# Eight-layer block with two expert layers on one core: fixed weight groups kept in SBUF, a state layer without small transfers, moved zeroing, and extra unread products

## What is computed

```python
x = x + cosine_attention(ln(x))       # layer 0, 8 heads of 8
x = x + experts(ln(x))                # layer 1: 160 experts, 8 per token, width 64
x = x + gated_linear_recurrence(ln(x))  # layer 2
x = x + experts(ln(x))                # layer 3, the same weights as layer 1
x = x + state_layer(ln(x))            # layer 4
x = x + channel_mix(ln(x))            # layer 5
x = x + rotary_attention(ln(x))       # layer 6, 16 heads of 8
x = x + channel_mix(ln(x))            # layer 7

def experts(x):
    probs = sigmoid(x @ router_w.T + bias); w, idx = top_k(probs, 8); w = 2.5 * w / sum(w)
    return sum_k w[k] * silu(x @ w_gate[idx[k]].T) @ w_down[idx[k]].T + silu(x @ gs.T) @ ds.T

def state_layer(x):
    u, z = split(x @ W_in + b_in)          # 256 channels each
    c = causal_conv4(u)
    h_t = tanh(c_t @ A + h_{t-1})          # 16 states, 256 steps in turn
    y_t = h_t @ C.T + Dp * c_t
    return (sigmoid(z) * y) @ W_out + b_out
```

## Time and profile before

| | |
|---|---|
| median of 3 runs | 2803.55 us (2802.51 to 2819.82) |
| profiled execution | 2797.68 us; its span in the trace 2795.8 us |
| mean granted clock of TensorE over the span | 0.738 of full speed |
| busy: PE, PEld, DVE, ACT, POOL | 60%, 40%, 49%, 35%, 39% |
| moved by DMA | 383.73 MB, mean 137 GB/s |
| attention of layer 0 | 0 to 205 us |
| experts of layer 1: routing, two halves | 205 to 456, 456 to 676, 676 to 905 us |
| layer 2 and the routing of layer 3 | 905 to 1306 us |
| experts of layer 3, two halves | 1306 to 1532, 1532 to 1770 us |
| state layer | 1770 to 2167 us |
| channel mix, rotary attention, channel mix | to 2217, to 2740, to 2796 us |

### The profile page before, as it was taken

One profiled execution on the slowest core, in us unless ns is written; L12 is line 12 of the kernel. 1 busy time (PEld: TensorE's weight loads), 2 busy tenths in 40 slices (PEclk: granted clock), 3 DMA queues, 4 the chain that ended last, 5 costly groups with the idle time before them and its releaser, 6 DMA issues.

```text
span 2795.8 us, 40361 instructions
## 1 busy us (share of the span) xinstructions
PE 1691.3 (60%) x13716; PEld 1106.9 (40%) x13716; DVE 1381.8 (49%) x3618; ACT 977.7 (35%) x1745; POOL 1080.0 (39%) x1177
## 2 busy tenths in 40 slices
PE   3775333676777454455686767541244468888885
PEld 2554222455555232243454555210022334444453
DVE  3648852322444577666422334552222665666746
ACT  3651001333333321221332323336692433344444
POOL 2000777762761773774770763575000300000001
PEclk9995556878778655555878878755555767899998
DMA  7991114999998111113998999311000000000001
GB/s 227 323 387 50 52 51 163 320 324 302 318 310 262 52 52 46 50 50 109 313 320 276 298 295 293 108 54 37 2 2 2 1 1 1 2 1 1 2 2 31
DMA packets 294229, 383.73 MB, mean 137 GB/s; under 512 B 70816, under 2 KB 163696, under 8 KB 293872
## 3 DMA queue, kind: packets, MB, share of 16 engines
q1 hardware_dynamic: 177280, 160.91, 18.6%
q10 hardware_dynamic: 83984, 153.13, 15.9%
q0 software_dynamic: 32768, 67.17, 7.8%
HBM read 231.64 MB, written 175.11 MB: 145 GB/s over the span
## 4 chain that ended last, share of the span: by engine, by line
PE 37%; DVE 18%; DMA 13%; ACT 12%; issue 8%; POOL 7%; SPq 4%; DVEq 0%; ACTq 0%; POOLq 0%
DMA arena<-expert_blocks 11%; ACT arena L965 5%; PE psum L1994 5%; PE psum L1984 5%; POOL slot_rows L1778 5%; PE psum L448 3%; SPq L1876 3%; PE psum L1957 3%; PE psum L1357 2%; PE psum L1338 2%; PE psum L432 2%; PE psum L1003 1%; PE psum L427 1%; ACT arena L1220 1%; DVE XN L590 1%
## 5 line engine op out<-in xcount | busy, mean ns | idle before, releaser
L1789 POOL DMA_INDIRECT arena<-slot_results,SLOTS x512 | 492.0, 961 | 428.6 <-DMA slot_results<-arena 235.9
L1778 POOL DMA_INDIRECT slot_rows<-arena,SLOTS x512 | 513.5, 1003 | 329.3 <-issue 329.3
L1748 DVE COPY arena<-psum 128x512 f32<-128x512 f32 x288 | 197.5, 690 | 629.7 <-PE psum L1994 624.9
L1984 PE MATMUL psum<-arena 128*64 128x128 f32 x2304 | 231.9, 333 | 225.7 <-DMA arena<-expert_blocks 196.4
L1832 ACT ACTIVATE arena<-psum 128x512 f32<-128x512 f32 x288 | 172.0, 597 | 478.2 <-PE psum L1957 439.9
L169 POOL TENSOR_SCALAR rstd<-mv 128x4 f32<-128x4 f32 x32 | 6.8, 212 | 725.7 <-DVE mv L577 725.2
L1957 PE MATMUL psum<-ident,arena 128*128 128x128 f32 x1152 | 224.7, 327 | 74.0 <-DMA arena<-slot_rows 73.5
L1984 PEld LDWEIGHTS psum<-arena 128*64 128x64 f32 x2304 | 148.0, 162 | 293.0 <-DMA arena<-expert_blocks 215.5
L1994 PE MATMUL psum<-arena 64*128 64x128 f32 x2304 | 248.9, 345 | 8.9 <-DVE arena L1748 8.8
L1994 PEld LDWEIGHTS psum<-arena 64*128 64x128 f32 x2304 | 186.2, 226 | 71.7 <-issue 71.0
L1839 ACT ACTIVATE arena<-psum 128x256 f32<-128x256 f32 x288 | 110.4, 383 | 267.2 <-PE psum L1984 265.6
(11 more groups left out here) (245 smaller groups left out, 3070.3 us busy)
## 6 DMA issues: line engine op xcount, KB each, us to landing
arena<-slot_rows ACTq DMA_DIRECT2D x288, 256.0 KB
slot_results<-arena ACTq DMA_DIRECT2D x288, 256.0 KB
arena<-expert_blocks SPq DMA_DIRECT2D x512, 96.0 KB
arena<-own_blocks SPq DMA_DIRECT2D x160, 256.0 KB
slot_rows<-zeros SPq DMA_DIRECT2D x2, 18432.0 KB, 79.8
own_blocks<-in_expert_w SPq DMA_DIRECT2D x4, 2560.0 KB, 22.6
slot_rows<-arena,SLOTS POOLq DMA_INDIRECT x512, 2.2
arena<-slot_results,SLOTS POOLq DMA_INDIRECT x512
```

The source lines that it names most:

```text
L1748: dve.tensor_copy(YSB[:, p].rearrange("p (c h) d -> p h c d", h=2), psum[:, first:first + 2, 0:256].rearrange("p h (c d) -> p h c d", c=2) ...
L1778: pool.indirect_dma_start(out=slot_rows[h], out_offset=bass.IndirectOffsetOnAxis(ap=slots_of(t, k), axis=0), in_=XNH[:, t], in_offset=None ...
L1789: pool.indirect_dma_start(out=GATHERED[:, t % TPI, k], out_offset=None, in_=slot_results[h], in_offset=bass.IndirectOffsetOnAxis(ap=slots_ ...
L1984: mm = pe.matmul(psum[lo:lo + INTER, 2 + 5 * (p % 2), o:o + P], gate_of(g, q), XSBT[:, p, P * q:P * q + P], start=True, stop=True, skip_gr ...
```

## The change

- **Fixed groups.** The weights of own groups 0 to 28 are put into SBUF (`STAYS`, 29 x 2 KB a partition) once, at the start, straight from the input; `own_blocks` keeps only the other 11. A half still has 72 groups; 43 of them are now brought by SP (`BROUGHT`: 32 by register, 11 own). The 4 buffers EWB serve the brought groups alone, so the load of one waits for the results of the fourth brought group before it, which is 6 or 7 groups back. The order of the own groups is mixed anew so that fixed ones stand evenly among the others. To make room, XSBT has 2 buffers instead of 4 (its writer already waited for the reader two groups back), YSB lies over routing buffers and the buffers of layer 2 over XSB, XSBT and HEB.
- **Two dense products a group.** `inner` issues two bfloat16 products of 256 columns ahead of its own four, into PSUM columns that nothing reads.
- **State layer.** A and C stand in SBUF as 8 padded copies each (A_AT, C_AT), so that PE's product lands on the partitions that the recurrence wants, accumulated in PSUM over four steps, and PE multiplies by C from the same layout. U16, H16 and the 32 small transfers of spreading and collecting go. DVE clears A_AT and C_AT and fills A_AT first (`spread_out`); SP fills C_AT. The sigmoid of the gate is written as tanh of half the argument. Recurrence 0 stands behind steps 4, 5 and 6 (64, 96, 96 steps of tanh). The sums of the last 16 tiles are dealt out anew: one tile in each of steps 0 to 3, four in each of steps 4 to 6.
- **Zeros.** POOL's four memsets for rotary attention stand in the channel mix of layer 5, after `inverse_deviations` of steps 2, 3, 4 and 5. Loops with one body are written out on POOL and PE there.

```diff
-        GROUP_ORDER = sorted(range(GROUPS), key=lambda n: (n + 0.5) / OWN_GROUPS if n < OWN_GROUPS else (n - OWN_GROUPS + 0.5) / MORE_GROUPS)
+        STAYING = 29
+        STAY = {n: n for n in range(STAYING)}
+        OWN_PLACES = sorted(range(OWN_GROUPS), key=lambda n: (n + 0.5) / STAYING if n in STAY else (n - STAYING + 0.5) / (OWN_GROUPS - STAYING))
+        GROUP_ORDER = sorted(range(GROUPS), key=lambda n: (OWN_PLACES.index(n) + 0.5) / OWN_GROUPS if n < OWN_GROUPS else (n - OWN_GROUPS + 0.5) / MORE_GROUPS)
+        BROUGHT = [g for g in range(GROUPS) if GROUP_ORDER[g] not in STAY]
...
-            for g in range(GROUPS):
-                n, p = GROUP_ORDER[g], g % UNROLL
-                if hr or g >= UNROLL:
-                    sp.wait_ge(c_y.sem, c_y.at(hr, 0, g - UNROLL + 1))
+            for m, g in enumerate(BROUGHT):
+                n, p = GROUP_ORDER[g], m % UNROLL
+                if m >= UNROLL:
+                    sp.wait_ge(c_y.sem, c_y.at(hr, 0, BROUGHT[m - UNROLL] + 1))
...
             def inner(g):
                 p = g % UNROLL
+                weights_in(g)
                 pe.wait_ge(c_xt.sem, c_xt.at(hr, 0, g + 1))
                 pe.wait_ge(c_he.sem, c_he.at(hr, 0, g - 1))
+                for _ in range(2):
+                    pe.matmul(psum[:, 2 + 5 * (p % 2), 256:512], identb[:], onesb[:].unsqueeze(1).broadcast_to([P, 2, P]),
+                              start=True, stop=True, skip_group_check=True)
...
+            def spread_out():
+
+                dve.memset(C_AT, 0.0).then_inc(m_at, 1)
+                dve.memset(A_AT, 0.0).then_inc(m_at, 1)
+                dve.tensor_scalar(B_HALF, b_in[:], 0.5, None, ALU.mult).then_inc(m_at, 1)
+                dve.wait_ge(m_at, 2)
+                for q in range(HALF):
+                    dve.tensor_copy(A_AT[:, q, :, STATE * q:STATE * q + STATE], m_a[:]).then_inc(m_at, 1)
+
+            spread_out()
             front(0)
-            for i in range(STEPS - 2):
-                step(i, [TILES // 2 + 2 * i], [TILES // 2 + 2 * i + 1])
-            step(STEPS - 2, [TILES - 4, TILES - 3], [TILES - 2, TILES - 1])
+            for i in range(HSTEPS):
+                step(i, [], [TILES // 2 + i])
+            for i in range(HSTEPS, STEPS - 1):
+                step(i, [TPI * i + TPI, TPI * i + TPI + 1], [TPI * i + TPI + 2, TPI * i + TPI + 3])
...
-                act.wait_ge(m_u_ps.sem, m_u_ps.at(0, i))
-                act.activation(U16[:, bass.ds(i * 2, 2), :], psum[0:STATE, 5, :].rearrange("p (b q) -> p b q", b=2), ACT.Copy).then_inc(m_u.sem, 1)
...
-                for e in range(E2):
-                    mm = pe.matmul(psum[0:STATE, 5, :], m_a[:, e, :], XCS[:, e].rearrange("p b q -> p (b q)"), start=(e == 0), stop=(e == E2 - 1))
+                pe.wait_ge(m_at, 3 + HALF)
+                for b in range(2):
+                    q = 2 * (i % HSTEPS) + b
+                    for e in range(E2):
+                        mm = pe.matmul(psum[:, 5 + i // HSTEPS, 0:SEQ], A_AT[:, q, e, :], XCS[:, e, b, :], start=(q == e == 0),
+                                       stop=(q == HALF - 1 and e == E2 - 1), skip_group_check=True)
...
-            pool.memset(VP2, 0.0).then_inc(r_zero, 1)
-            pool.memset(QS2, 0.0).then_inc(r_zero, 1)
-            pool.memset(KS2, 0.0).then_inc(r_zero, 1)
-            pool.wait_ge(r_zero, 3)
-            pool.memset(KS2[:, :, MROW:MROW + 3], 1.0).then_inc(r_zero, 1)
             pool.wait_ge(r_zero, 4)
```

More of the change, by code:

```diff
@@ L805, in ffn_scalar, with ffn_gpsimd @@
                     previous(i + 2)
-        def ffn_gpsimd(pool, layer):
+        def ffn_gpsimd(pool, layer, between=()):
             r, run = front_run(layer), earlier(layer)
-            with pool.Fori(0, STEPS) as i:
+            for i in range(STEPS):
                 inverse_deviations(pool, i, r)
+                if 2 <= i < 2 + len(between):
+                    between[i - 2](pool)
         def ffn_tensor(pe, layer):
@@ L849, in program @@
         m_a = weight("m_a", [P, E2, STATE])
-        m_ct = weight("m_ct", [STATE, E2, P])
         m_d = weight("m_d", [P, E2])
@@ L901, in convolve @@
             def convolve(i):
-                dve.wait_ge(m_u_ps.sem, m_u_ps.before(0, i))
+                if i:
+                    dve.wait_ge(m_u_ps.sem, m_u_ps.before(0, i))
                 dve.wait_ge(m_xc.sem, m_xc.before(0, i))
@@ L1012, in output @@
                 for e in range(E2):
-                    mm = pe.matmul(psum[:, 1 + e, :], m_ct[:, e, :], H16[:, bass.ds(i * 2, 2), :].rearrange("p b q -> p (b q)"), start=True, stop=True)
+                    for b in range(2):
+                        mm = pe.matmul(psum[:, 1 + e, SEQ * b:SEQ * b + SEQ], C_AT[:, 2 * (i % HSTEPS) + b, e, :], H[:, i // HSTEPS, :],
+                                       start=True, stop=True, skip_group_check=True)
                 mm.then_inc(m_y_ps.sem, 1)
@@ L1021, in output @@
                 mm.then_inc(m_out.sem, 1)
+            pe.wait_ge(m_ct, 16 * HALF)
+            pe.wait_ge(m_xp.sem, m_xp.end(0))
             for g in range(2):
-                pe.wait_ge(m_gather, 16 * HALF * (g + 1))
-                with pe.Fori(g * STEPS // 2, (g + 1) * STEPS // 2) as i:
+                pe.wait_ge(m_h[g], SEQ + 1)
+                for i in range(g * HSTEPS, (g + 1) * HSTEPS):
                     output(i)
@@ L1530, in program @@
         blocked = semaphore("blocked")
+        stays = semaphore("stays")
         e_stat = signal("e_stat", HTILES, HALVES)
@@ L1958, in transposes, with own_of @@
                 mm.then_inc(c_tr.sem, 1)
+            def own_of(g):
+                n = GROUP_ORDER[g]
+                return STAYS[:, STAY[n]] if n in STAY else EWB[:, BROUGHT.index(g) % UNROLL].rearrange("p q c -> p (q c)")
             def gate_of(g, q):
```

132 lines of the change are left out of this document (76 added, 56 removed).

## The result

The changed kernel takes **2571.6 us** (median of 4 runs, 2566.1 to 2577.2) where the kernel before takes 2804.2 beside it (2802.5 to 2819.8): a ratio of 0.916, 95% interval 0.912 to 0.920. The forecast was 2659 in a range of 2605 to 2712; the gain is 233 us where 145 were forecast.

| stretch | before | after | difference |
|---|---|---|---|
| up to the first expert half | 459.2 | 457.3 | -1.9 |
| first layer of experts | 443.2 | 355.5 | -87.7 |
| layer between and routing | 405.6 | 408.3 | +2.7 |
| second layer of experts | 459.3 | 356.2 | -103.1 |
| from there to the end | 1028.5 | 992.5 | -36.0 |

What follows compares the result with a forecast made beforehand. The prediction took DMA bandwidth as the bound of the expert halves, with load lateness close by. Fixed groups -118, state layer -18, zeros -9.5 + 1 from 2797.7 gave 2653, plus 5.9 for the median: 2659 us, range 2605 to 2712.

Steps and rivals of the forecast that it cites:

- The fixed groups: Expert halves: 29 weight groups no longer loaded per half cut DMA's busy time from 838 to 759 us; 118 us less.
- 759 / 0.98 + 20 = 795: Four expert halves: remaining DMA busy time at a 0.98 share, plus 5 us lost per half, gives 795 us.
- DMA runs free: Rival, expert halves: they run at 353 GB/s, POOL's gathers bounding second halves; 720 to 760 us, total 2584 to 2624; chance 0.15.
- The share stays: Rival, expert halves: loads late for another reason, such as rows behind stores; halves 827 us, total 2691; chance 0.2.
- nothing from the fixed groups: Rival, expert halves: packets slow down as others take their place, only small edits count; total 2777 us; chance 0.04.
- The signs that were to show the forecast right: Profile after: halves 190 to 205 us, DMA share 0.95 or more, weight waits nearly gone, clock above 0.9.
- PE at half clock: Rival, expert halves: gaps keep PE's clock low, a group costs 3.7 us; total 2860 us at 85% of groups; chance 0.03.
- they hide behind DMA: Expert halves: dense products cost zero while fewer than 35% of groups run at half clock; otherwise up to 72 us.
- State layer: -18 forecast: State layer: convolution, norm, table loads, tanh steps and collection save time, less spreading and last outputs; net -18 us (-11 to -20).
- the terms for steps 0 to 3 and the start: State layer: step 0 convolution -3.1, sum before step 1's norm -2.4, table loads in steps 1 to 3 -3.9, spreading +4.9.
- +0.9: State layer, last four outputs: wider weight loads and DVE's three-operand gate add 0.9 us, an estimate.
- -9.5 + 1: Moved memsets: POOL's norm at rotary's start 9.5 us earlier; channel mix 1 us longer (0 to 4).

Runs made afterwards that it cites:

- the run with bytes and no reach: Changed kernel, but SP issues a brought load only when the group four back has its results, as in the kernel before: 2777.5 us, ratio 0.991.

## Why the prediction was wrong

**The fixed groups: -118 forecast, -190.8 measured.** The measured 2571.6 lies below the range and below every rival. The step that failed reads "759 / 0.98 + 20 = 795": I took the busy time of DMA as an amount of work and its share as a capacity. The price of the bytes in busy time was right, as the run with bytes and no reach shows (78 us), and it decided nothing: that run gained 0.9%, the small edits included. Two things showed it in the earlier trace rows and in my own text: the loop of four groups that lasts 12.2 us, and a load of 7 us inside it. The chain of the kernel before, 596 to 615 us, shows one round: results, the start of the next load's issue, its transfer, and the two groups' products up to the results that free the buffer again.

```profile
599.50 0.67 PE psum L1994 x8
600.25 0.30 SPq L1872
602.59 4.66 DMA arena<-expert_blocks
607.30 0.66 PE psum L1984 x8
607.96 1.10 PE psum L1994 x8
609.06 1.04 PE psum L1957 x4
610.10 1.05 PE psum L1984 x8
611.16 0.80 PE psum L1994 x8
```

From 600.17 to 611.96 it is 11.8 us: 2.4 until the last transfer is under way, 4.7 until it lands, 4.7 of PE. Such a ring lasts 12.2 us on average (that is 220 / 18, no second measurement), and taking bytes away does not shorten it unless the single load gets shorter. I saw it, wrote "two limits lie close together", and then costed the change by the other one. The share of 0.93 was the ring's doing. Eight buffers and not one byte less give 161 us of the 190.

The second part of the error is that busy time is not fixed. With the same packets it fell from 820 to 737 us once loads were queued ahead. The rival "DMA runs free" had nearly the right size for the halves, 193 us less at best against 190.8, and I gave it 0.15; its 2584 was still 12 us too slow, mostly by the state layer. Its reasons were half right: POOL's gathers do bound the second halves, as it says; the rate of 353 GB/s that it used was too low (390 to 400 are reached), and the first halves lose by DVE at their start what they gain there. That these two errors nearly cancel is luck.

- *The share stays*, *nothing from the fixed groups*: both speak of DMA as the bound and fall with it. Removing bytes alone did leave the time nearly as it was.
- The signs that were to show the forecast right nearly all came: the share (0.97 to 0.98), the waits for weights gone, the clock above 0.9. Only the halves' length (172 to 178 us for 190 to 205) told the two mechanisms apart, as eight buffers with all bytes in place give nearly the same signs (share 1.01, waits for weights 15.7 us, clock 0.89 to 0.93).
- *PE at half clock*: did not come. The clock rose to 0.93 to 0.95 once the waits were gone, and does so without the dense products (0.90 to 0.94). The earlier trace rows do not yet show its return; the same timeline does, some 4.3 us behind the start at 620.64.
- By the rule of the Trainium skill (DMA: Bandwidth & Descriptors, section Queues, rings and completion order) PE was to wait for rows in place of weights. The trace of the first half after shows 0.4 us of such waits behind the first group and 7.4 in the second, that with eight buffers and all bytes 6.9 in the first: it fits the rule, at a price of a few us a half.

**Dense products: 0 forecast, about 0 measured in the change** (687.9 against 699.1 in the halves of one profile each, nothing in the ratio). In a kernel bound by the ring they cost 26 us, so they bring nothing in either. The condition under which I had let them be free ("they hide behind DMA") was the wrong one: PE's part of the ring was on the path.

**State layer: -18 forecast, -28.4 measured.** Head +4.9, as forecast (two memsets of 1.76 us each, so the price by ACT's copy was the nearer one). From the first transposed tokens to the first tanh step -12.8 where the terms for steps 0 to 3 and the start give about -11; from there to the last tanh step -5.1 for -6.3; the collection -6.5, as forecast. The term that was mis-sized is "+0.9" for the last four outputs: they take 9.0 us less, since products over 128 rows bring PE's clock up and products over 16 did not. Of the 10.4 us by which the sum was off, 9.9 are in this term.

**Zeros: -9.5 + 1 forecast.** The start of rotary gained 9.4. "+1 (0 to 4)" in channel mix was 4.7, another 1.4 us of the 6.1 there coming with the changed state layer (a table load of ACT, 1.28 us, which the trace of before does not have there: ACT now enters channel mix with tanh's table in place of the sigmoid's). The rule that the forecast weighed, the Trainium skill, SBUF — State Buffer, section Who interferes with whom (some VectorE work takes an SBUF port that GpSimd needs too, and one of the two stands still), is confirmed by the scaling of 3.66 us beside a memset of 3.51. I had called it untested for want of a row and left it out of the sum. Its price of 10.5 was too high, as the scaling comes some time after the memset has begun.

**The sum.** Of the 87 us between 2659 and 2571.6, 72.8 are the fixed groups and 10.4 the state layer; channel mix and rotary's start take back 5.2. Another 5.9 are the distance between the median and the profiled execution, which the forecast added; after the change the two are equal. The rest, some 4 us, lies in stretches that have no term; behind the start of rotary attention the profiles differ by up to 6 us from run to run.

## What to carry to other kernels

Before costing a change of bytes, follow one buffer round: issue, landing, use, release. If that ring, divided by the number of buffers, is as long as the period, the busy share of DMA is an outcome, and more buffers, an earlier release or a shorter round will help, but not fewer bytes in other loads; a cheap test is to remove the bytes and keep the waits. Work that "fills PE's waits" is free only off the ring. And where a memset of GpSimd is moved out of the way, ask what VectorE does in the new place.

## What the hardware showed that I had not expected

- DMA's busy time for the same packets is shorter when more is queued: 67.10 MB in 214.2 us at a share of 0.94 in the kernel before (201 us), 67.07 MB in 184.6 us at 1.01 with eight buffers (186 us), 390 to 400 GB/s in the best slices. Why a packet takes less time is open.
- 32 rows against 128 in the same products decide whether PE's clock stays above its half level (3.78 against 2.05 us for the next 16 products).
- In the profiles of the experiments where before took 3413 us or more, PE stood still while POOL issued its indirect transfers, in waits for nothing that the profile shows ("issue"), though DMA was nearly idle, and it ran as usual once POOL was done. This is PE and its largest waits from 590 to 642 us in the run with 32 rows, beside which the rows above from 705 us show it fed. The kernel with eight buffers has the same 294229 packets in 3324 us as in 2639. One chip showed this in one set and not in a later one. The cause is open.

```profile
590.00:642.00 52.00, 3.88 (x22) 2.02 (x18) 0.69 (x1) 0.98 (x2) 39.24 (x41) 0.50 0.18 63
...
PE psum L2030 <- issue: 26.9, 1, 26.9
...
PE psum L2044 <- issue: 17.0, 1, 17.0
```
